# Attention kernel: denominators copied out by ScalarE, second queries moved, low parts of the lead on GpSimd, identity products in the heads of eight

## The reference

```python
x = x + _L0_attn_ref(_layernorm(x, axis=-1), ...)            # stage a0: 16 heads of 64, keys are x's 1024 rows
x = x + _L0_xattn_ref(_layernorm(x, axis=-1), ctx_768, ...)  # stage c0: 16 heads of 64, keys are the 6404 context rows
x = x + _L0_ffn_ref(_layernorm(x, axis=-1), ...)             # stage f0: routed experts
x = x + _L1_attn_ref(_layernorm(x, axis=-1), ...)            # stage a1: 16 heads of 8, rotary
x = x + _L1_xattn_ref(_layernorm(x, axis=-1), ctx_768, ...)  # stage c1: 8 heads of 64, context keys
x = x + _L1_ffn_ref(_layernorm(x, axis=-1), ...)             # stage f1: routed experts
```

## Time and profile before

| | us |
|---|---|
| median of 3 runs | 4218.35 (4216.9 to 4227.25) |
| profiled execution, whole time | 4227.08 |
| its span, first to last instruction | 4225.3 |

### The profile page before, as it was taken

One profiled execution on the slowest core, in us unless ns is written; L12 is line 12 of the kernel. 1 busy time (PEld: TensorE's weight loads), 2 busy tenths in 40 slices (PEclk: granted clock), 3 DMA queues, 4 the chain that ended last, 5 costly groups with the idle time before them and its releaser, 6 DMA issues. The chain is left out here.

```text
span 4225.3 us, 72943 instructions
## 1 busy us (share of the span) xinstructions
PE 4034.8 (95%) x26942; PEld 2193.3 (52%) x26942; DVE 2724.2 (64%) x3418; ACT 1828.5 (43%) x2125; POOL 2787.3 (66%) x1342
## 2 busy tenths in 40 slices
PE   7999899999999999999999999999899999999998
PEld 4444455554545545555555556733355555554558
DVE  5666867667676676766767743368666767667533
ACT  3444244444444444444444443346344444444443
POOL 4667187878877788877878892000077878878950
PEclk9999999999999999999999999969999999999999
DMA  1000000000000000000000000100000000000001
GB/s 37 6 6 2 5 2 2 2 2 2 2 2 3 2 3 2 2 3 2 2 1 1 2 1 24 40 1 1 4 2 2 2 2 2 2 1 2 1 14 33
DMA packets 25457, 23.95 MB, mean 6 GB/s; under 512 B 6322, under 2 KB 19107, under 8 KB 25123
## 3 DMA queue, kind: packets, MB, share of 16 engines
q1 hardware_dynamic: 23666, 17.05, 1.4%
q10 hardware_dynamic: 1456, 2.46, 0.2%
HBM read 18.97 MB, written 0.52 MB: 5 GB/s over the span
## 5 line engine op out<-in xcount | busy, mean ns | idle before, releaser
L427 POOL TENSOR_TENSOR c_SUM<-c_SUM,c_PR 128x896 f32<-128x896 f32 (+2 forms) x1170 | 2449.9, 2094 | 446.1 <-ACT c_PR L498 353.4
L594 DVE TENSOR_REDUCE c_MX<-c_XB 128x2 f32<-128x1024 f32 (+2 forms) x1156 | 1391.7, 1204 | 844.4 <-PE c_XB L794 844.2
L498 ACT ACTIVATE c_PR<-c_S 128x1024 f32<-128x1024 f32 (+1 forms) x1224 | 1194.6, 1024 | 1610.5 <-PE c_S L829 1529.9
L847 PE MATMUL c_O<-c_PR,c_V 128*64 128x512 f32 (+1 forms) x4896 | 1178.3, 599 | 0.0
L847 PEld LDWEIGHTS c_O<-c_PR,c_V 128*64 128x64 f32 (+1 forms) x4896 | 316.8, 136 | 538.1 <-issue 416.5
L829 PE MATMUL c_S<-c_SH,c_ONE 64*128 64x512 f32 x2448 | 486.8, 392 | 0.0
L794 PE MATMUL c_XB<-c_KHM,c_QH 64*128 64x512 f32 x1632 | 369.3, 447 | 26.6 <-DVE c_MX L594 21.1
L794 PEld LDWEIGHTS c_XB<-c_KHM,c_QH 64*128 64x128 f32 x1632 | 154.7, 185 | 380.8 <-DVE c_MX L594 208.8
L829 PE MATMUL c_S<-c_QH,c_KHM 64*128 64x512 f32 x1728 | 349.4, 400 | 0.3 <-DVE c_SH L584 0.3
L829 PE MATMUL c_S<-c_QL,c_KHM 64*128 64x512 f32 x1728 | 345.2, 394 | 0.0
L829 PE MATMUL c_S<-c_QH,c_KLM 64*128 64x512 f32 x1728 | 343.9, 393 | 0.0
(11 more groups left out here) (324 smaller groups left out, 4730.6 us busy)
## 6 DMA issues: line engine op xcount, KB each, us to landing
f_W<-in_L_w SPq DMA_DIRECT2D x34, 256.0 KB, 2.7
CTX<-in_ctx ACTq DMA_DIRECT2D x12, 192.0 KB, 4.6
c_WQ<-in_L_xattn_Wq SPq DMA_DIRECT2D x12, 64.0 KB, 1.9
c_WO<-in_L_xattn_Wo SPq DMA_DIRECT2D x12, 64.0 KB, 1.8
c_WK<-in_L_xattn_Wk SPq DMA_DIRECT2D x12, 48.0 KB, 1.7
c_WV<-in_L_xattn_Wv SPq DMA_DIRECT2D x12, 48.0 KB, 1.8
X<-in_x SPq DMA_DIRECT2D x1, 512.0 KB, 6.7
a_WQ<-in_L_attn_Wq SPq DMA_DIRECT2D x8, 64.0 KB, 2.0
```

Of the source, the lines that this page charges most:

```text
L427: pool.tensor_tensor(out[0:kp], out[0:kp], tile[0:kp], ALU.add).then_inc(summed, 1)
L498: act.activation(PR[0:kp, u % BUFS, :, :].rearrange("p h q -> p (h q)"), S[u % 2][0:kp, :], ACT.Exp)\
L594: dve.tensor_reduce(MX[:, q:q + tiles, :, column], bank[:].rearrange("p (h k) -> p h k", h=2) [:, :, 0:tiles * m].rearrange("p h (q k) -> ...
L847: last = pe.matmul(O[ROWS[h], :], V[pair.par][0:kp, t, ROWS[h]], PR[0:kp, u % BUFS, h, :], start=t == 0, stop=t == TILES - 1)
```

## The change

Four edits.

1. D jobs: ACT copies SIDE whole into RDEN and frees SIDE; DVE takes the reciprocals in place in RDEN, in four parts as before, on a new semaphore `reciprocals`, for which `normalise` waits. ACT first waits that RDEN's last reader is done (`normal`).
2. In a0 the job Q1 moves from half 0, group 2, behind K1, to half 1, group 0, behind V0.
3. In the lead, ACT copies SIDE a second time, whole, into the first three PR buffers in turn (`leave_whole`), and frees SIDE. POOL makes the low part from it by a subtraction (semaphore `low_made`). DVE does nothing for Q and K in the lead. ACT's fourth and later copies wait for the subtraction three back; the first scores wait for all of them.
4. In a1, four identity products behind M0 and ten behind the scores of the first tile.

```diff
@@ -82,9 +82,9 @@
                 self.side[0][free[i * (len(free) - 1) // (len(jobs) - 1)], 0] = job
         else:
-            self.side[0] = {(0, 0): ("Q", 0), (0, 1): ("K", 0), (1, 0): ("D", 1), (2, 0): ("K", 1), (2, 1): ("Q", 1),
+            self.side[0] = {(0, 0): ("Q", 0), (0, 1): ("K", 0), (1, 0): ("D", 1), (2, 0): ("K", 1),
                             (3, 0): ("Y", 1), (3, 1): ("M", 1)}
-            self.side[1] = {(0, 0): ("V", 0), (1, 0): ("D", 0), (2, 0): ("V", 1), (3, 0): ("Y", 0), (3, 1): ("M", 0)}
+            self.side[1] = {(0, 0): ("V", 0), (0, 1): ("Q", 1), (1, 0): ("D", 0), (2, 0): ("V", 1), (3, 0): ("Y", 0), (3, 1): ("M", 0)}
@@ -240,7 +240,8 @@
-        inverted = sem("inverted")
+        low_made = sem("low_made")
+        inverted, reciprocals = sem("inverted"), sem("reciprocals")
@@ -302,6 +303,10 @@
+
+        def whole(i):
+
+            return PR[:, i % 3, 0, :]
 
         def q_at(par, half):
             return QH[2 * par + half], QL[2 * par + half]
@@ -406,6 +411,16 @@
+                for i, job in enumerate(QK_LEAD):
+                    pool.wait_ge(side_free, plan.lead.index(job) + 1)
+                    if job[0] == "Q":
+                        high, low = [x[:] for x in q_at(0, job[1])]
+                    else:
+                        m = plan.chunk_keys(job[1])
+                        kh, kl, at = k_at(0, job[1])
+                        high, low = kh[:, at:at + m], kl[:, at:at + m]
+                    pool.tensor_tensor(low, whole(i)[:, 0:low.shape[1]], high.bitcast(F32), ALU.subtract).then_inc(low_made, 1)
+
@@ -436,15 +451,29 @@
 
             @block.scalar
             def _(act):
+                def leave_whole(job, bank, by):
+                    i = QK_LEAD.index(job)
+                    if i >= 3:
+                        act.wait_ge(low_made, i - 2)
+                    act.activation(whole(i)[:, 0:bank.shape[1]], bank, ACT.Copy, scale=by).then_inc(side_free, 1)
+
                 def side(pair, job, end):
-                    if job[0] not in ("Q", "K", "V"):
+                    if job[0] not in ("Q", "K", "V", "D") or absent(pair, job):
                         return
                     n = number(pair, job, end)
                     to = of_pair(pair, job)
                     act.wait_ge(side_done, n + 1)
+                    if job[0] == "D":
+                        if not (to.first and job[1] == 0):
+
+                            act.wait_ge(normal, 2 * to.p + job[1])
+                        act.activation(RDEN[:], SIDE[:], ACT.Copy).then_inc(side_free, 1)
+                        return
                     if job[0] == "Q":
                         qh, _ = q_at(to.par, job[1])
                         act.activation(qh[:], SIDE[:], ACT.Copy, scale=scale).then_inc(side_act, 1)
+                        if pair is None:
+                            leave_whole(job, SIDE[:], scale)
                     elif job[0] == "K":
                         c, m = job[1], plan.chunk_keys(job[1])
                         kh, _, at = k_at(to.par, c)
@@ -452,6 +481,8 @@
 
                             act.wait_ge(s_done, plan.step(pair.p, 1, 4 * c + 3) + 1)
                         act.activation(kh[:, at:at + m], side_bank(pair, job)[:, 0:m], ACT.Copy).then_inc(side_act, 1)
+                        if pair is None:
+                            leave_whole(job, side_bank(pair, job)[:, 0:m], 1.0)
                     else:
                         if not pair.first:
 
@@ -537,23 +568,24 @@
 
                     n = plan.job(pair.p, ("D", half), end)
                     for i in parts:
-                        if i == 0:
-                            dve.wait_ge(side_done, n + 1)
+                        if i == 0 and not absent(pair, ("D", half)):
+                            dve.wait_ge(side_free, n + 1)
                         q = slice(i * P, (i + 1) * P)
                         if absent(pair, ("D", half)):
                             if i == 3:
+                                dve.wait_ge(side_done, n + 1)
                                 dve.wait_ge(side_free, n)
                                 dve.engine_nop().then_inc(side_free, 1)
                             continue
-                        each = dve.reciprocal(RDEN[:, q], SIDE[:, q])
+                        each = dve.reciprocal(RDEN[:, q], RDEN[:, q])
                         if i == 3:
-                            each.then_inc(side_free, 1)
+                            each.then_inc(reciprocals, 1)
 
                 def normalise(pair, half, end=False):
                     if absent(pair, ("D", half)):
                         return
                     to = of_pair(pair, ("D", half))
-                    dve.wait_ge(side_free, plan.job(pair.p, ("D", half), end) + 1)
+                    dve.wait_ge(reciprocals, 2 * to.p + half + 1)
                     dve.wait_ge(evac, 2 * to.p + half + 1)
                     dve.tensor_tensor(OT[:], OT[:], RDEN[:], ALU.mult).then_inc(normal, 1)
 
@@ -636,10 +668,9 @@
                 for kind, job in LEAD:
                     if kind == "max":
                         maximum(job, lead_bank(job), plan.maxima[0][job])
-                    elif kind == "side":
-                        if job[0] == "M":
-                            dve.wait_ge(filled, FILLS)
-                            shift(plan.half_maxima)
+                    elif kind == "side" and job[0] == "M":
+                        dve.wait_ge(filled, FILLS)
+                        shift(plan.half_maxima)
                         side(None, job, False)
 
                 def period(pair, end):
@@ -812,6 +843,7 @@
                             pe.wait_ge(side_free, plan.job(pair.p, ("M", 1), end) + 1)
                         elif pair.first:
                             pe.wait_ge(filled, FILLS)
+                            pe.wait_ge(low_made, len(QK_LEAD))
                             pe.wait_ge(side_free, len(plan.lead))
                         else:
                             pe.wait_ge(side_free, plan.job(pair.p - 1, ("M", 0)) + 1)
@@ -1201,6 +1233,7 @@
                 keep_busy(pe, O, ident, 6)
                 pe.wait_ge(lead_free, UNITS // 2)
                 side(("M", 0))
+                keep_busy(pe, O, ident, 4)
                 for k in range(AHEAD):
                     maximum(k)
                 for p in range(PERIODS):
@@ -1215,6 +1248,8 @@
                         for k in units[2:3]:
                             maximum(k)
                         tiles(p, t)
+                        if (p, t) == (0, 0):
+                            keep_busy(pe, O, ident, 10)
                         if job is not None and job[0][0] in "KQ":
                             side(job)
                         for k in units[3:]:
```

## The result

The kernel after takes 4202.47 us in the median of 5 runs (4192.26 to 4205.87) against 4218.35 of the kernel before: ratio 0.9957, 95% interval 0.9943 to 0.9972, faster by 0.4%. Forecast were 4179 and a range of 4168 to 4201. The direction was right, the gain was less than half of the forecast, and the median lies just above the range. Its trace shows the same long multiplications, and a1 at 258.6 us. Runs of one kernel differ by 10 us and more to each side: in all, 69 runs of the kernel before lie between 4211.66 and 4245.07. They go with the mean granted clock of the run, 0.985 in the run of 4211.73 and 0.973 in one of 4243.85.

What follows compares the result with a forecast made beforehand. PE bounds the loops of c0 and a0, DVE c0's lead, PE at half clock part of a1. 4227.1 - 11.9 - 7.6 - 15.0 - 1.2 + 4.8 - 17 = 4179.2 us; range 4168 to 4201, forecast's own 4170 to 4190.

Steps and rivals of the forecast that it cites:

- a0: Pair loop of a0: waits for reciprocals go, -11.9 us; moving Q1 gives -7.6; its lead gives -1.2.
- Rival (b): In a0: the removed waits turn into waits for maxima; 4189 us in all, chance 0.08.
- The leads: Leads of c0 and c1: low parts leave DVE's chain, 4.53 us a chunk left, -15.0 us for both.
- Rival (e): Leads: no shorter, as a POOL subtraction takes over 4.5 us and ACT waits for it; +15, 4194; chance 0.03.
- D by ScalarE in c: Loops of c0 and c1: the copy starts reciprocals 0.53 us late, 0.22 reaches PE in 22 jobs, +4.8 us.
- rival (d): In c and a0: reciprocals with SBUF source stand behind POOL's sums, 0.51 us lost each; +67, 4246; chance 0.03.
- Rival (c): D jobs: reciprocals are faster from SBUF than PSUM, so c gives nothing back; 4174 us, chance 0.10.
- a1: In a1: identity products around the thin stretch at M0 keep or restore full clock; -21.3 + 4 = -17 us.
- rival (a): In a1: the slow clock comes back behind the ten products; 4189 or 4201 us, chance 0.27.
- The base: Sum starts from the profiled 4227.1 us, not the 4218.35 median; two run levels were laid to a1's slow stretch.

Runs made afterwards that it cites:

- a1 with more products: Kernel after without the copy in c0 and c1, plus ten more identity products in a1 behind the second group's scores: 4179.12 us, ratio 0.9882.
- the shifted one: Kernel before with eight more identity products at the end of c0 (13 instead of 5), nothing changed in a1: 4219.26 us, ratio 0.9998.
- the sum waiting: Kernel after, where in c0 and c1 one POOL sum waits for the multiplication OT times RDEN: 4187.36 us, ratio 0.9919.
- DVE made late: Kernel before with an idle 80-column reciprocal on DVE ahead of each D's third and fourth reciprocals in c0 and c1: 4268.96 us, ratio 1.0093.

## Why the prediction was right or wrong

**a0: right, a little small.** Forecast for the stage: -11.9, -7.6 and -1.2 for its lead, -20.7. Traces: -22.5 and -1.4; alone, -18.2 in the median, and in its trace c0, where nothing was changed, gave 10.3 back. A pair takes 46.3 us in the trace (forecast 46.6). Rival (b) did not come: waits for maxima 1.4 us against 2.8.

**The leads: right, a little small.** Forecast -15.0; traces -17.4. Alone, with a0's lead, -17.0 where 16.2 was forecast. A chunk takes 4.52 us (4.53), a subtraction 1.27 (1.2). Rival (e) is out.

**D by ScalarE in c: wrong, the step that failed.** The sum had +4.8, "0.53 late", of which 0.22 reach PE. That part was too dear: a half without collision and fall is 0.1 longer, and the wait that was to go from 0.47 to 0.7 us is 0.54. But I followed the delay through "two reciprocals and a maximum" and stopped before the next instruction of DVE, the multiplication, which in before started 0.01 us ahead of POOL's sum. Where 0.1 us of the delay was left, it turned that order round, and the wait of 1.29 us is a new one, one unit of maxima further on, which the sum did not have. Measured: +15.6 for the copy alone (6 to 19); in the trace of the kernel after some 14.2 are the multiplication. The row was in my hands, for rival (d) drew on the 1.19 us of OT times RDEN in a0, but put the mechanism on the reciprocals, which have one source in SBUF and take 1.76 a pair as before. The multiplication has two, and I did not ask when it starts. The rival had the right sign and mechanism, the wrong instruction, and a price of 67 us.

The Trainium skill (SBUF — State Buffer, "Who interferes with whom") has both halves of this: a DVE instruction with two SBUF inputs contends with a GpSimd instruction that reads SBUF, and the order of issue decides who is blocked. I had used only its sentence on one input. The trace agrees: 2.60 us behind a sum, 0.67 ahead of it.

**Rival (c): out.** The reciprocals from SBUF take 921 ns in the mean, those from PSUM 920 (60 each in c0). The 65 ns that the Trainium skill (VectorE: DVE Perf Modes, the section on the errata) would have them faster are not there.

**a1: right in the trace by luck, wrong in its cause.** The earlier trace rows were read as the kernel's own. Forecast -17, trace -17.5, and 258.6 us in the second trace. But the kernel after without the products has 258.6 too, and the kernel before with eight identity products more in c0 261.2. The products do not decide what the clock does in a1: with them there are traces of 282.8 and 274.8, of the size of rival (a). In the 17 traces the long spell goes with the moment at which the clock first falls behind M0; why it falls at that moment stays open. The second failed step is that a spell seen in one profiled execution was taken for the kernel's and given to one edit as its price. By the median of the edit alone the term is +1.9, by its interval -10 to +7.

**The base.** Starting from 4227.1, with "two levels some 9 us apart" laid to the spell, was wrong too. Both executions of before that were profiled have the full spell and take 4227 and 4231, but 67 of the 69 runs fill the room from 4212 to 4238, with no gap over 3 us, and two lie near 4244.

**What the sum left out** is the clock at the turns of c. In the trace 9 more falls cost some 14 us, by the estimate above. Kernels with no copy in c have them in c0 (37 and 44 us at 0.50, a0 alone and a1 with more products) and in c1 (the shifted one), so the copy is not needed for them. All five traces of c1 with the copy in c have 23 to 27 us at 0.50 there, and eleven of twelve without it 3 to 13. With the sum waiting, which has the copy but not the long multiplication, it is 23. Whether the copy makes them likelier, or only moves the turns to a worse moment, stays open.

From the ratios of the edits alone, of 4218: a0 -21.5, leads -16.5, copy in c +12.7, products -1.3, together -26.6. The two measurements of the kernel after give -18 (12 to 24) and -33 (24 to 43). The parts add up within the intervals.

## What to carry over

Where an edit delays an engine by a fraction of a microsecond, follow it through every later instruction of that engine, and look at the starts of two-input work on DVE against POOL's: an order held by 0.01 to 0.04 us was worth 1.5 us a half and more. A wait that is hidden is no reason for a copy: in c nobody waited for SIDE, and the versions without the copy there are the shortest. Before the price of a stretch at half clock goes into a sum, see whether it is there in the traces of several kernels whose stage is the same; a second execution of before still had it.

## What the runs showed of the hardware

- DVE's multiplication of two SBUF tiles and POOL's addition from SBUF hardly overlap: whichever starts second waits for the other (0.67 against 2.60 us on DVE, 2.12 against 2.64 on POOL), with starts 0.07 and 0.01 us apart. In the kernel with DVE made late, all 22 multiplications of the two pair loops start 0.3 to 0.5 us into a sum, and each ends 0.55 us behind it.
- Falls of the clock come in rows, from turn to turn. In c1 of the kernel after, long multiplication and fall together lengthen a half from 129.8 us in the mean to 133.0, and six falls follow each other, each at the next turn (3297.9, 3431.0, 3564.1). That one fall brings the next is not shown: in c0 of the same kernel the rows break off, and with DVE late five halves of c1 in a row have the long multiplication and no fall.
- Half clock can cost next to nothing: 51 us of it in the lead of c1 cost 3.3, and 14 us more in a1 cost no more than the fourteen identity products that were left out there.
